# Flamingo layer kernel on one core: new block order in the first stage, products over both heads at once, row sums through PSUM, statistics of x2 on ScalarE

## What is computed

```python
kv = einsum('bhil,bhjl->bijhl', c_, c_)            # c_ = c as (b, head, 8, L)
y = irfft(rfft(kv, n=1024) * rfft(ssm_kernel, n=1024))[..., :L]   # causal convolution
out = y + kv * D
out = einsum('bijhl,bhil->bjhl', out, layernorm(x))
x = x + tanh(g_xattn) * out
t = layernorm(x)
scores = softmax(t @ gate_w.T); top 2 of 16 experts
y = sum over the chosen experts of swiglu(t, w1, w3, w2) * weight
z = swiglu(t, sw1, sw3, sw2)                       # shared part
out = x + tanh(g_ffn) * (y + z)
```

## Time and profile before

| | us |
|---|---|
| median of 3 runs | 743.66 |
| lowest, highest | 741.99, 745.06 |
| the profiled execution | 741.57 |
| its span | 739.8 |
| TensorE busy in the span | 717.1 |
| VectorE busy | 568.5 |
| ScalarE busy | 459.4 |
| GpSimd busy | 363.4 |

### The profile page before, as it was taken

How to read it: one execution, slowest core, us unless ns; L and a number is a source line. 1 busy time by engine, 2 the same in 40 slices (tenths; PEclk the granted TensorE clock), 3 DMA queues, 4 the chain that set the end, 5 groups by cost and what they waited for, 6 DMA issues and landing times.

```text
span 739.8 us, 15553 instructions
## 1 busy us (share of the span) xinstructions
PE 717.1 (97%) x4602; PEld 676.3 (91%) x4602; DVE 568.5 (77%) x1111; ACT 459.4 (62%) x659; POOL 363.4 (49%) x190
## 2 busy tenths in 40 slices
PE   3999999999999999999999999999999999999998
PEld 3999999999998999899989999988989999999997
DVE  7899999999965578428899588848987699679942
ACT  6575757575432222126878588847885789578931
POOL 4999888887401065042435433543634354434320
PEclk9999999999999999999999999999999999999999
DMA  6678687877522122463667577766565764432101
GB/s 231 215 239 288 218 272 216 279 218 253 186 85 60 29 43 29 144 197 90 161 201 218 131 232 210 198 176 168 145 182 160 176 193 90 74 68 46 30 1 57
DMA packets 48404, 114.88 MB, mean 155 GB/s; under 512 B 7472, under 2 KB 8624, under 8 KB 48336
## 3 DMA queue, kind: packets, MB, share of 16 engines
q1 hardware_dynamic: 35792, 89.67, 37.1%
q0 software_dynamic: 12544, 24.40, 17.9%
HBM read 157.78 MB, written 29.26 MB: 253 GB/s over the span
## 4 chain that ended last, share of the span: by engine, by line
PE 69%; DVE 13%; DMA 6%; issue 5%; ACT 3%; SPq 1%; ACTq 1%; POOL 1%; DVEq 1%; POOLq 0%
PE pair L1303 19%; PE bank L1303 15%; PE pair L1328 12%; PE pair L1234 8%; PE bank L1328 6%; PE bank L1185 4%; PE pair L1311 3%; DMA out<-ys,slot_info 3%; DMA raw<-in_weights 2%; PE bank L1245 2%; DVE prod L829 2%; DVE bank L834 2%; DVE x L800 2%; DVE w_lo L1150 1%; DVE rows L841 1%
## 5 line engine op out<-in xcount | busy, mean ns | idle before, releaser
L1150 DVE TENSOR_TENSOR w_lo<-raw,w_hi 128x1408 fp32r<-128x1408 f32 x94 | 148.5, 1621 | 47.0 <-ACT w_hi L733 47.0
L1441 POOL DMA_INDIRECT out<-ys,slot_info x47 | 80.6, 1714 | 120.6 <-ACT ys L721 87.3
L1428 POOL DMA_INDIRECT tn<-t_rows,slot_info x47 | 75.5, 1605 | 123.1 <-DVE tT_lo L888 90.6
L733 ACT ACTIVATE w_hi<-raw 128x1408 fp32r x94 | 124.6, 1374 | 2.1 <-issue 1.4
L1234 PE MATMUL pair<-kv_hi,toep_hi 128*128 128x288 f32 x320 | 100.6, 314 | 1.7 <-DMA toep_lo<-kpad_lo 1.4
L1234 PE MATMUL pair<-kv_lo,toep_hi 128*128 128x288 f32 x320 | 95.3, 298 | 0.0
L1234 PE MATMUL pair<-kv_hi,toep_lo 128*128 128x288 f32 x320 | 95.1, 297 | 0.0
L1155 DVE TENSOR_TENSOR w_lo<-raw,w_hi 128x1536 fp32r<-128x1536 f32 x47 | 82.3, 1752 | 4.5 <-ACT w_hi L740 4.5
L1379 POOL TENSOR_TENSOR kv_lo<-kv,kv_hi 128x2304 fp32r<-128x2304 f32 x15 | 77.3, 5153 | 5.9 <-ACT kv_hi L625 5.9
L740 ACT ACTIVATE w_hi<-raw 128x1536 fp32r x47 | 69.3, 1474 | 0.1
L829 DVE TENSOR_TENSOR prod<-pair,q 128x256 f32<-128x256 f32 x128 | 53.4, 417 | 15.1 <-PE pair L1234 9.6
(11 more groups left out here) (223 smaller groups left out, 2009.3 us busy)
## 6 DMA issues: line engine op xcount, KB each, us to landing
raw<-in_weights SPq DMA_DIRECT2D x94, 704.0 KB
raw<-in_weights SPq DMA_DIRECT2D x47, 768.0 KB
toep_hi<-kpad_hi SPq DMA_DIRECT2D x15, 512.0 KB, 4.6
toep_lo<-kpad_lo SPq DMA_DIRECT2D x15, 512.0 KB, 6.2
cx<-in_ctx SPq DMA_DIRECT2D x15, 384.0 KB, 6.3
stage<-in_weights SPq DMA_DIRECT2D x16, 272.0 KB, 6.7
xt<-in_x SPq DMA_DIRECT2D x16, 256.0 KB, 6.4
xr<-in_x SPq DMA_DIRECT2D x16, 256.0 KB, 6.6
```

Of the source, the lines that this page charges most:

```text
L733: act.activation(w_hi[s % 2][:, a:b], raw[:, bass.ds(half + a, b - a)], ACT.Copy).then_inc(hi_ok[n_], 1)
L1150: dve.tensor_tensor(w_lo[s % 2][:, a:b], raw[:, bass.ds(half + a, b - a)], w_hi[s % 2][:, a:b].bitcast(F32), ALU.subtract).then_inc(lo_ok[ ...
L1428: pool.indirect_dma_start(out=tn[o % 3][:], out_offset=None, in_=t_rows, in_offset=bass.IndirectOffsetOnAxis(ap=slot_info[:, 3 * i:3 * i + ...
L1441: pool.indirect_dma_start(out=out, out_offset=bass.IndirectOffsetOnAxis(ap=rows, axis=0), in_=ys[o % 2][:], in_offset=None, bounds_check=R ...
```

## The change

In turns 1 to 15 the blocks are taken in the order 0, 3, 1, 2, on TensorE, VectorE and ScalarE alike; turn 0 keeps 0 to 3. Where the code before had `lb` as the place in the turn, it now has `k`, and `block_of(t, k)` gives the block. The places of `gate`, `logits_copy` and the rest in the programs of TensorE and VectorE are the same, by place in the turn.

The layout of rows in a tile is now head, channel, batch, so that products of both heads are one instruction. `products` waits for both heads' matmuls. It has three products (384 and 128 elements into `prod`, 512 into `ps_rows`), then an add of 256 in place in `ps_rows`, one of 256 into `half_sum`, and one of 256 into `rows`. `sum_rows` has three transposes, two of `rows` and one of `prod`.

x2's statistics are taken on ScalarE, by the same two passes as x's. x's statistics on ScalarE are of tile t+2 instead of t+1, and stand between `norm_x` and `q_copy`.

```diff
-PROD_STEPS = 6
+PROD_STEPS = 3
+SUMROWS = 2
+TURN = (0, 3, 1, 2)
...
+        def block_of(t, k):
+
+            return k if t.within(0, 1) else TURN[k]
...
+            def stats(src, mv, ok, t):
+
+                p = t.odd
+                act.activation(spent[:], src[p][:], ACT.Copy, scale=-1.0 / L, accum_out=mv[p][:, 0:1]).then_inc(ok, 1)
+                wait(act, ok, t * 2 + 1)
+                act.activation(spent[:], src[p][:], ACT.Square, bias=mv[p][:, 0:1],
+                               accum_out=mv[p][:, 1:2]).then_inc(ok, 1)
+                wait(act, ok, (t + 1) * 2)
...
             def std_x2(t):
-                wait(act, stat2, (t + 1) * 2)
-                act.activation(sd2[t.odd][:, 0:1], mv2[t.odd][:, 1:2], ACT.Sqrt, bias=small[:, 0:1]).then_inc(std2, 1)
+                wait(act, x2_ok, t + 1)
+                wait(act, rstd2, (t - 1) * 2)
+                stats(x2, mv2, stat2, t)
...
                 if not first and not last:
                     split_kv_hi(t + 1)
-                    std_x(t + 1)
                 if not first:
                     std_x2(t - 1)
...
+                if not t.within(TILES - 2, TILES):
+                    std_x(t + 2)
+                if not last:
                     q_copy(t + 1)
...
                 dve.scalar_tensor_tensor(x2[p][:], ps_o[:], small[:, 1:2], xr[p][:],
                                          ALU.mult, ALU.add).then_inc(x2_ok, 1)
-                wait(dve, x2_ok, t + 1)
-                stats(x2, st2, mv2, stat2, t)
...
+            def products(t, k):
...
+                wait(dve, conv_ok, t * 8 + 2 * k + 2)
+                dve.tensor_tensor(view(w, BATCH, [[n, 2], [HB + BATCH, 3], [1, HB]]),
+                                  view(y, HB, [[512, 2], [HB, 3], [1, HB]]),
+                                  view(z, qo, [[GW, 2], [0, 3], [1, HB]]), ALU.mult).then_inc(prod_ok, 1)
+                dve.tensor_tensor(view(w, 2 * n, [[HB, 2], [HB // 2, 2], [1, HB // 2]]),
+                                  view(y, 4 * HB, [[512, 2], [0, 2], [1, HB // 2]]),
+                                  view(z, qo + HB // 2, [[GW, 2], [HB // 2, 2], [1, HB // 2]]),
+                                  ALU.mult).then_inc(prod_ok, 1)
+                wait(dve, rows_ok, t * 4 + k)
+                dve.tensor_tensor(view(ps_rows, 0, [[HB, 2], [P, 4], [1, HB]]),
+                                  view(y, 0, [[512, 2], [HB, 4], [1, HB]]),
+                                  view(z, qo, [[GW, 2], [BATCH, 4], [1, HB]]), ALU.mult).then_inc(prod_ok, 1)
+                wait(dve, prod_ok, (t * 4 + k + 1) * PROD_STEPS)
+                m = SUMROWS * P
+                dve.tensor_tensor(ps_rows[:, m:], ps_rows[:, m:], view(w, 2 * HB, [[HB, 2], [n, 2], [1, HB]]),
+                                  ALU.add).then_inc(half_ok, 1)
+                dve.tensor_tensor(half_sum[:], ps_rows[:, 0:m], view(w, 0, [[HB, 2], [n, 2], [1, HB]]),
+                                  ALU.add).then_inc(half_ok, 1)
+                wait(dve, half_ok, (t * 4 + k + 1) * 2)
+                dve.tensor_tensor(rows[par][:], ps_rows[:, m:], half_sum[:], ALU.add).then_inc(rows_ok, 1)
...
-                for r in range(PRODROWS):
-                    part = (rows if r < BLOCKS else prod)[lb % 2]
-                    mm = pe.matmul(ps_o[:, lb * P:(lb + 1) * P], part[:, r * P:(r + 1) * P], ident[:],
-                                   is_transpose=True, start=(r == 0), stop=(r == PRODROWS - 1))
+                last = prod[k % 2][:, 8 * HB:]
+                for r in range(SUMROWS + 1):
+                    part = rows[k % 2][:, r * P:(r + 1) * P] if r < SUMROWS else last
+                    mm = pe.matmul(ps_o[:, lb * P:(lb + 1) * P], part, ident[:],
+                                   is_transpose=True, start=(r == 0), stop=(r == SUMROWS))
```

More of the change, by code:

```diff
@@ L217, in program @@
         prod = sb2("prod", [P, PRODROWS * P], F32, one)
-        rows = sb2("rows", [P, L], F32, one)
+        rows = sb2("rows", [P, SUMROWS * P], F32, one)
+        half_sum = sb("half_sum", [P, SUMROWS * P], F32, one)
         spent = sb("spent", [P, L], F32, one)
@@ L569, in _ @@
             act.activation(small[:, 3:4], small[:, 0:1], ACT.Sqrt)
+            def stats(src, mv, ok, t):
[5 more added lines that the diff above has]
+                wait(act, ok, (t + 1) * 2)
             def std_x(t):
-                p = t.odd
-                wait(act, x_in[p], (t.half() + 1) * 16)
+                wait(act, x_in[t.odd], (t.half() + 1) * 16)
                 wait(act, rstd1, (t - 1) * 2)
[L576 to L581, removed]
+                stats(xt, mv1, stat1, t)
+                act.activation(sd1[t.odd][:, 0:1], mv1[t.odd][:, 1:2], ACT.Sqrt, bias=small[:, 0:1],
                                scale=1.0 / L).then_inc(std1, 1)
             def std_x2(t):
-                wait(act, stat2, (t + 1) * 2)
-                act.activation(sd2[t.odd][:, 0:1], mv2[t.odd][:, 1:2], ACT.Sqrt, bias=small[:, 0:1]).then_inc(std2, 1)
+                wait(act, x2_ok, t + 1)
+                wait(act, rstd2, (t - 1) * 2)
+                stats(x2, mv2, stat2, t)
+                act.activation(sd2[t.odd][:, 0:1], mv2[t.odd][:, 1:2], ACT.Sqrt, bias=small[:, 0:1],
+                               scale=1.0 / L).then_inc(std2, 1)
             def norm_x(t):
@@ L607, in q_copy @@
                 wait(act, q_turned, t + 1)
[L608 to L611, removed]
+                act.activation(view(q[p][:], 0, [[2 * GW, BLOCKS], [GW, 2], [1, HB]]),
+                               view(ps_q, 0, [[P, BLOCKS], [HB, 2], [1, HB]]), ACT.Copy).then_inc(q_ok, 1)
+                act.activation(view(q[p][:], HB, [[2 * GW, BLOCKS], [GW, 2], [1, HB // 2]]),
+                               view(ps_q, 0, [[P, BLOCKS], [HB, 2], [1, HB // 2]]), ACT.Copy).then_inc(q_ok, 1)
             def tT_copy(t):
@@ L671, in turn @@
                     std_x(t + 1)
+                if first:
                     split_kv_hi(t + 1)
@@ L809, in scale_x2 @@
                 wait(dve, rstd2, t * 2 + 1)
[L810 to L838, removed]
-                                      view(qq, qo + 4 * G, [[4 * G, 2], [G, 4], [1, BATCH]]), ALU.mult).then_inc(prod_ok, 1)
-                wait(dve, prod_ok, (t * 4 + lb + 1) * PROD_STEPS)
-                dve.tensor_tensor(rows[par][:], ps_rows, prod[par][:, 0:L], ALU.add).then_inc(rows_ok, 1)
@@ new lines, in scale_x2 @@
+                dve.tensor_scalar(mv2[p][:, 2:3], mv2[p][:, 0:1], sd2[p][:, 1:2], None,
+                                  ALU.mult).then_inc(rstd2, 1)
+            def products(t, k):
+                par = k % 2
+                y, z, w = ps_conv[par][:], q[t.odd][:], prod[par][:]
+                qo, n = block_of(t, k) * 2 * GW, 4 * HB
+                wait(dve, summed, t * 4 + k - 1)
+                if k == 0:
+                    wait(dve, q_ok, (t + 1) * 2)
+                wait(dve, conv_ok, t * 8 + 2 * k + 2)
[18 more added lines that the diff above has]
+                dve.tensor_tensor(rows[par][:], ps_rows[:, m:], half_sum[:], ALU.add).then_inc(rows_ok, 1)
@@ L1222, in conv @@
                                 wait(pe, kvl_ok, t + 1)
-                        if t.within(0, 1) and lb == 1:
+                        if t.within(0, 1) and k == 1:
                             pe.wait_ge(toep_in[0], 32)
                             pe.wait_ge(kvl_first, 2)
-                        if t.within(0, 1) and lb == 2:
+                        if t.within(0, 1) and k == 2:
                             pe.wait_ge(kvl_ok, 1)
-                        wait(pe, prod_ok, (t * 4 + lb - 1) * PROD_STEPS)
+                        wait(pe, prod_ok, (t * 4 + k - 1) * PROD_STEPS)
                     for mb in range(lb + 1):
@@ L1466 @@
     x, c = a("x"), a("ctx_2048")
-    x_rows = x.reshape(BATCH, TILES, 2, HD, L).transpose(1, 3, 2, 0, 4).reshape(ROWS, L)
+    x_rows = x.reshape(BATCH, TILES, 2, HD, L).transpose(1, 2, 3, 0, 4).reshape(ROWS, L)
     cc = c.reshape(BATCH, TILES, 2, HD, BLOCKS, P)[..., ::-1].transpose(1, 5, 4, 2, 3, 0)
@@ L1505 @@
     got = run(nc, [arrays], core_ids=[0]).results[0]["out_0"]
-    return got.reshape(TILES, HD, 2, BATCH, L).transpose(3, 0, 2, 1, 4).reshape(BATCH, HEADS * HD, L)
+    return got.reshape(TILES, 2, HD, BATCH, L).transpose(3, 0, 1, 2, 4).reshape(BATCH, HEADS * HD, L)
```

25 lines of the change are left out of this document (10 added, 15 removed).

## The result

The changed kernel took 758.86 us (median of 6 runs, 755.34 to 761.39), the kernel before 743.91 beside it (6 runs, 741.99 to 745.83). The ratio is 1.0213, 95% interval 1.0186 to 1.0241: slower, by 14.95 us. The forecast was 755, range 748 to 762. The profiled execution took 755.34 us with a span of 753.5; the one before 741.57 with 739.8.

The account below looks back on a forecast made before the run. TensorE was taken to bound the first stage before; after the change, a loop through the router's wait, 13.0 us a turn against 12.25. Terms 0.6-0.1+9.8+0.8 = 11.1 us on the median 743.66 gave 754.8, called 755, range 748 to 762.

Parts of the forecast that it names:

- The turn: First stage, end of VectorE's last `rows` add to the next turn's: 13.04 us, called 13.0, against 12.25 before.
- the forecast's list: Ten terms from `rows` to `rows`, through sum, block 3, router's matmuls, logits, three blocks of products and scales: 13.04 us.
- The path over TensorE: Alternative to the scales and third products, through a sum and block 2's 18 matmuls: as long, 13.0 us a turn.
- The block of products: VectorE's six new instructions per block: 2.53 us to the next start, 2.62 to the last add's end, against 2.20.
- the dearer rival: VectorE's block dearer, as by in-place work in one PSUM bank: 2.8 us, a turn of 13.85, 767 us; chance 0.11.
- The wait for the logits: VectorE's logits copy waits for TensorE's router matmuls, behind block 3's 24 matmuls: 1.4 us, 14 times.
- TensorE's idle time: TensorE waits ahead of two of its sums: 13.0-11.38 = 1.6 us a turn in all.
- a turn would take at most 12.25-0.87 = 11.38: TensorE's turn if it stayed the bound, 0.87 us of transposes leaving; the forecast said it doesn't stay the bound.
- TensorE bounds the stage, with VectorE little behind: First stage before the change, turns 1 to 14: TensorE busy 169.41 us of 171.80, VectorE 155.60.
- What hides: ScalarE's x2 statistics done at 5.1 us, VectorE asking at 7.3, cover 2.2; x's landing loop, 12.2, costs nothing.
- The sum: Whole first stage: turn 0 0.6, turn 1 -0.1, turns 2 to 14 9.8, turn 15 0.8; together 11.1 us slower.
- The clock: TensorE's clock stays at 1.00; the rival, a fall from short idle pieces, gave 795 us, chance 0.03.

Follow-up runs that it names:

- the one moved instruction: Changed kernel with VectorE's copy of the router's logits moved behind the products at place 1: 743.67 us, ratio 1.0011 to the kernel before.
- the later kernels: Kernel before with block order 0, 1, 3, 2 (737.04 us), with x2's statistics on ScalarE (737.23), or with both (737.17).

## Why the prediction was right, point by point

- **The turn.** Forecast 13.04, called 13.0; measured 13.15 to 13.20, in turn 2 and the last three 13.02. The terms in the order of the forecast's list, from turn 8: 0.06, 0.30, 3.26, 0.96, 0.16, 0.13, 2.53, 0.64, 2.51, 2.60. Mis-sized were two: the start behind the router's matmuls was 0.16, not 0.04, and the logits 0.13, not 0.10. The 0.04 was taken from a product behind the convolution; the row at hand was of another pair of instructions. Together they are 0.15, the last two blocks take 0.04 of it back, and the two sums differ by 0.11. The path over TensorE that the prediction called as long, 13.0, comes to 12.9 by its own terms (13.04-3.17+3.00), and the trace has the fourth products start without a wait.
- **The block of products.** Forecast 2.53 from the spacing of starts; measured 2.53, 2.51, and 2.60 to the end of the last. The add in place in PSUM lasted 0.43 against 0.41 for the other, so the dearer rival had no ground. By the cost per instruction in the Trainium skill's table ("VectorE: DVE Perf Modes", "The TRN2 errata") the prediction had an estimate of 2.62; the trace shows 2.51 to 2.53, since neighbours overlap (durations 0.56 and 0.28, starts 0.47 and 0.20 apart).
- **The wait for the logits.** Forecast 1.4 us 14 times; the trace has 14 and 19.9 us, 1.4 each (1.57 in turn 8, 1.2 in its neighbours). That the loss comes through this wait is shown by the one moved instruction.
- **TensorE's idle time.** Forecast 1.6 a turn, in two pieces. Its recorded waits in turns 2 to 14 are 22.1/13 = 1.7. Against 11.92-0.87 = 11.05, an estimate of TensorE's work from the later kernels, it is 2.1. A step that failed is the 12.25 in "a turn would take at most 12.25-0.87 = 11.38": it took a whole turn for TensorE's work. "At most" was right, and the time did not hang on it, because the loop was the longer.
- **What bounded the kernel before.** "TensorE bounds the stage, with VectorE little behind" was half wrong. A loop over TensorE, ScalarE and VectorE set 12.25, and x2's statistics were in it. The prediction booked their leaving only in VectorE's own work. In the changed kernel it was indeed worth nothing, but in the kernel before it is worth some 6 us (ratio 0.9919).
- **What hides.** x2's statistics on ScalarE started at 121.67 and its square root ended at 123.56; VectorE asked at 125.78. Cover 2.2, as forecast:

```profile
121.67 0.63 ACT L581 ACTIVATE spent<-x 128x512 f32<-128x512 f32 x1 [1.12 <-DVE x L808]
...
123.27 0.29 ACT L598 ACTIVATE sd<-mv,small 128x1 f32<-128x1 f32 x1
```

- **The sum.** Turns 2 to 14: +11.48 for 9.8, 0.13 a turn: 0.04 is the rounding of 13.04 to 13.0, the rest the start and the logits. Turn 15 +0.88 for 0.8, turn 1 -0.04 for -0.1. In all the first stage lost 13.6 where 11.1 was forecast, and the medians 14.95: right in range and mechanism, a quarter short in size. Turn 0 +1.26 for 0.6: no single cause is shown, since turn 0 ended between 25.43 and 28.04 in the profiled executions of all these kernels, also of those whose turn 0 is the same.
- **The clock.** Forecast to stay, with 0.03 for the fall. TensorE idled twice a turn, 0.78 and 0.99 us in turn 8, and the granted clock read 1.00 over the stage. The rule of the Trainium skill ("TensorE: Matmul & The Clock Gate", "A second HAM failure mode: psum-queue depth-cycling") would have made it go back and forth; idle pieces of this length and spacing did not do that here.

## What to carry to other kernels

Before you add up what an engine has to do, write down the loops: from an event in one turn to the same event in the next, over every engine whose instruction waits in program order. An instruction of 0.16 us that waits for another engine holds up everything queued behind it, here 15 us in all; when work on the other engine is reordered, look at what stands ahead of the thing it waits for. And a share of 98.6% busy is no proof that an engine is the bound: matmul durations overlap, and a third of a microsecond a turn, 2.7%, was to be had by relieving another engine.

## What was unexpected in the hardware

A VectorE instruction that waits for TensorE started 0.04 us after the last matmul's recorded end behind the 288-column matmuls (116.94+0.29 to 117.27 in the kernel with the logits moved), but 0.16 behind the router's 16-column ones (122.96 to 123.12). The matmuls' ends are modelled, so it may be the model and not the chip; as a term of a sum it counts all the same.

VectorE's first products of turns 5, 7, 9 and 11, each the first turn of a pass of the program's loop, started 0.26 to 0.34 us behind the `rows` ahead of them, with nothing that the profile shows to wait for. That is so in six of these kernels, four times each; in the two kernels where these products stand in the turn's loop (block order 0, 1, 2, 3 or 0, 1, 3, 2) these four turns are some 0.44 us longer than the others.

The second stage is the same code in all these kernels, and yet from the last `rows` to the end of the span it was 528.2 to 532.9 us over their thirteen profiled executions. That is as much as some of the effects, and why turns were compared here, and whole times only by medians.
